# Second attention of a six-layer block: fp32 probabilities as the moving operand over banded fp32 values, and the rotation of queries and keys on GpSimd

## The reference, cut to what matters

```python
q = x @ Wq;  k = x @ Wk;  v = x @ Wv                  # 16 query heads, 4 key/value heads, head width 8
q = _rope(q, cos(ang), sin(ang));  k = _rope(k, cos(angk), sin(angk))
scores = einsum('bhqd,bhkd->bhqk', q, k) / sqrt(128)  # 256 x 256 per head, no mask
p = softmax(scores, axis=-1)
o = einsum('bhqk,bhkd->bhqd', p, v)
return o.transpose(0, 2, 1, 3).reshape(B, S, D) @ Wo
```

## Time and profile before

| | before |
|---|---|
| median of 3 runs | 1822.4 us (1815.99 to 1823.57) |
| profiled execution, span of its instructions | 2151.2 us |
| time of the profiled execution around the span | none is given |
| attention 1: first scores to the last add | 1219.7 to 1595.5 us of the span |
| VectorE / ScalarE / TensorE busy, 1400 to 1444 us | 94% / 85% / 80% |
| granted TensorE clock there | 0.50 |
| GpSimd busy there | 69% |

### The profile page before, as it was taken

The page is one execution under the profiler, slowest core; times in us unless marked ns, Lnnn a source line. Parts: engine busy times, 40 slices in busy tenths (PEclk is TensorE's granted clock), DMA queues, the critical chain, the costliest instruction groups (busy, mean ns, idle before and its releaser), DMA issues.

```text
span 2151.2 us, 34449 instructions
## 1 busy us (share of the span) xinstructions
PE 1289.1 (60%) x11544; PEld 930.5 (43%) x11545; DVE 1132.4 (53%) x2864; ACT 781.4 (36%) x1164; POOL 970.1 (45%) x1052
## 2 busy tenths in 40 slices
PE   2496578736921424987743387777750513997762
PEld 1495466526820113976511144444430201986621
DVE  6445677672478101423533699889978200333442
ACT  1243366613410001533211188888850100443310
POOL 0623155523225764034462267667633766024464
PEclk9997799957955766999775555555555755998885
DMA  7232144102200112444310000000000111444321
GB/s 303 82 88 73 57 159 152 57 12 86 76 25 31 48 67 67 149 137 123 92 48 22 11 2 2 3 2 2 2 1 20 48 66 52 137 141 129 108 74 49
DMA packets 100126, 150.60 MB, mean 70 GB/s; under 512 B 21520, under 2 KB 54928, under 8 KB 99216
## 3 DMA queue, kind: packets, MB, share of 16 engines
q1 hardware_dynamic: 58768, 75.30, 11.0%
q0 software_dynamic: 20480, 41.98, 6.7%
q10 hardware_dynamic: 20736, 31.47, 4.3%
HBM read 74.16 MB, written 74.45 MB: 69 GB/s over the span
## 4 chain that ended last, share of the span: by engine, by line
PE 33%; DVE 19%; another core or an unknown queue 17%; issue 15%; ACT 4%; POOL 4%; SPq 4%; DMA 3%; ACTq 1%; DVEq 0%; POOLq 0%
PE PS L910 6%; PE PS L932 3%; PE PS L847 3%; SPq L1349 2%; PE PS L300 2%; PE PS L302 2%; PE PS L301 2%; PE PS L1793 2%; PE PS L918 2%; POOL AREA L1100 2%; POOL slots_top L626 2%; DVE AREA L1959 2%; DVE X L1123 1%; DVE XN L409 1%
## 5 line engine op out<-in xcount | busy, mean ns | idle before, releaser
L1100 POOL DMA_INDIRECT AREA<-results_top,ROW x320 | 305.3, 954 | 516.5 <-DMA results_top<-AREA 330.1
L626 POOL DMA_INDIRECT slots_top<-XN,ROW x320 | 318.2, 995 | 319.0 <-DVE ROW L580 185.8
L742 DVE SCALAR_TENSOR_TENSOR AREA<-PS,AREA 128x512 f32<-128x512 f32 x64 | 43.8, 691 | 323.2 <-issue 181.2
L910 PE MATMUL PS<-WGU,AREA 128*128 x768 | 192.7, 396 | 13.7 <-ACT AREA L974 13.7
L1754 POOL TENSOR_TENSOR AREA<-AREA 128x1024 f16<-128x1024 f32 x64 | 151.4, 2365 | 91.6 <-ACT AREA L1894 91.4
L1011 DVE SCALAR_TENSOR_TENSOR AREA<-PS,AREA 128x512 f32<-128x512 f32 x96 | 66.4, 692 | 218.0 <-ACT AREA L985 170.9
L712 ACT ACTIVATE AREA<-PS 128x512 f32<-128x512 f32 x64 | 38.1, 598 | 373.7 <-remote 293.9
L1983 DVE TENSOR_REDUCE AREA<-PS 128x4 f32<-128x1024 f32 x128 | 156.1, 1219 | 25.4 <-PE PS L1781 24.7
L1887 ACT ACTIVATE AREA<-PS,AREA 128x1024 f32<-128x1024 f32 x128 | 142.7, 1115 | 53.5 <-PE PS L1793 53.5
L910 PEld LDWEIGHTS PS<-WGU,AREA 128*128 128x128 f32 x768 | 146.3, 201 | 32.9 <-ACT AREA L974 15.0
L932 PE MATMUL PS<-WD,AREA 128*128 x768 | 112.5, 293 | 53.3 <-DVE AREA L1006 46.2
(11 more groups left out here) (261 smaller groups left out, 3636.4 us busy)
## 6 DMA issues: line engine op xcount, KB each, us to landing
AREA<-slots_top SPq DMA_DIRECT2D x96, 256.0 KB
results_top<-AREA ACTq DMA_DIRECT2D x96, 256.0 KB
slots_top<-ZERO SPq DMA_DIRECT2D x24, 512.0 KB, 3.1
AREA<-slots_top SPq DMA_DIRECT2D x48, 128.0 KB
results_top<-AREA ACTq DMA_DIRECT2D x48, 128.0 KB
AREA<-query_rows SPq DMA_DIRECT2D x48, 128.0 KB, 2.9
slots_top<-XN,ROW POOLq DMA_INDIRECT x320
AREA<-results_top,ROW POOLq DMA_INDIRECT x320
```

The lines of the kernel that those rows point to most:

```text
L626: nc.gpsimd.indirect_dma_start(out=L.xs[q], out_offset=bass.IndirectOffsetOnAxis(ap=ROW[:, n:n + 1], axis=0), in_=XN[:, t * D:(t + 1) * D] ...
L910: ins = nc.tensor.matmul(o, XTF[:, v, j * P:(j + 1) * P], w, start=True, stop=True)
L1100: nc.gpsimd.indirect_dma_start(out=slots[L.tag][u][:, c * D:(c + 1) * D], out_offset=None, in_=L.ys[g * GT // L.tiles], in_offset=bass.Ind ...
```

## The change

It touches attention 1 alone.

- The split of the probabilities is gone (`phi`, `plo`, `PB1`). `PF1` is now fp32 and double, one for even and one for odd tiles.
- `values` has the roles swapped: the stationary operand is `V32`, for each of 8 tiles and 4 key/value heads 128 keys x 32 columns in fp32, of which 8 hold v, one holds 1.0 and the rest 0; the moving operand is `PF1`, 256 columns in fp32. Head g writes partitions 32g to 32g+32 of bank 6, so that the four matmuls of a call use four different bands of columns of the array. 16 matmuls for a tile, in four calls, run in the turn after the tile's exponentials.
- The result lies by head and query: ScalarE copies the whole bank (512 columns) to `OS`, TensorE transposes it back in four fp32 transposes (`values_turned`, bank 7), VectorE's `norm` has two operations, one fp32 transpose (into bank 0), a copy to `OT` and one fp32 matmul with Wo (`AOF`, rows in another order) follow. The add to x comes a turn later, and the turns go on for one more.
- `rope` moves from VectorE to GpSimd: ScalarE copies columns 0 to 320 of the projections to `PJQ` (in `XN`, which is free then), and GpSimd does two multiplications and an addition, each part behind a `carry_wait`. ScalarE's copy of v gives it in fp32; there is no low half.

The diff, cut to its core:

```diff
-        PF1 = area([4, 1024], F32)
-        PB1 = [area([4, 1024], F16) for _ in range(2)]
-        OS = area([16 * 17], F32)
+        PF1 = [area([4, 1024], F32) for _ in range(2)]
+        OS = area([4 * P], F32)
+        V32 = area([8, 4, 32], F32)
+        PJQ = XN[:, 0:640].rearrange("p (a b) -> p a b", b=320)
...
-            for c in range(NT - 5, NT + 2):
+            for c in range(NT - 5, NT + 3):
                 turn(0, c)
...
+            def rope(i, c):
+                t = i * 8 + c
+                wait(pool, b_pj, t + 1)
+                wait(pool, b_rope, t)
+                wait(pool, b_pack, t - 1)
+                carry_wait()
+                nc.gpsimd.tensor_tensor(RT[:, 0, :], PJQ[:, c % 2, 0:160], COS[:, c % 2, :], ALU.mult)
+                nc.gpsimd.tensor_tensor(RT[:, 1, :], PJQ[:, c % 2, 160:320], SIN[:, c % 2, :], ALU.mult
+                                        ).then_inc(b_rstep.sem, 1)
+                wait(pool, b_rstep, t + 1)
+                carry_wait()
+                nc.gpsimd.tensor_tensor(RF[:, c % 2, :], RT[:, 0, :], RT[:, 1, :], ALU.add).then_inc(b_rope.sem, 1)
...
                 if tile_exists(i, c + 4):
                     pack_k(i, c + 4)
-                if tile_exists(i, c - 1):
-                    plo(i, c - 1, 3)
-                if tile_exists(i, c + 4):
                     pack_q(i, c + 4)
-                if tile_exists(i, c):
-                    plo(i, c, 1)
+                if tile_exists(i, c + 5):
+                    rope(i, c + 5)
...
-            def values(i, c, g):
+            def values(i, c, n):
                 t = i * 8 + c
-                wait_split(pe, i, c, g)
-                if g == 0:
-                    wait(pe, b_oc, t)
-                for r in range(4):
-                    o = (4 * g + r) * 17
-                    for k in range(2):
...
-                        nc.tensor.matmul(banks(6)[:, o:o + 17], p[0], v, start=k == 0, stop=False)
-                        ins = nc.tensor.matmul(banks(6)[:, o:o + 9], p[1], v[:, 0:9], start=False, stop=k == 1)
+                odd, k = divmod(n, 2)
+                wait(pe, b_exp, 4 * t + 4)
+                wait(pe, b_oc, t)
+                for g in range(4):
+                    at = odd * 512 + k * 256
+                    ins = nc.tensor.matmul(banks(6)[32 * g:32 * (g + 1), odd * 256:(odd + 1) * 256],
+                                           V32[:, (c // 2 * 2 + k) % 8, g, :], PF1[c % 2][:, g, at:at + 256],
+                                           start=k == 0, stop=k == 1)
                 ins.then_inc(b_pv.sem, 1)
+
+            def values_turned(i, c):
+                t = i * 8 + c
+                wait(pe, b_oc, t + 1)
+                wait(pe, b_on, t)
+                for odd in range(2):
+                    for half in range(2):
+                        at, r = (odd * 2 + half) * P, 2 * half + odd
+                        ins = nc.tensor.transpose(banks(7)[:, r * P:(r + 1) * P], OS[:, at:at + P], IDF[:, :])
+                ins.then_inc(b_vt.sem, 1)
...
-                    before = c - 1 if g < 3 else c
-                    if tile_exists(i, before):
-                        values(i, before, (g - 3) % 4)
+                    if g > 0 and tile_exists(i, c - 1):
+                        values(i, c - 1, g - 1)
+                    if g == 3 and tile_exists(i, c - 1):
+                        values(i, c - 1, 3)
...
+                    if g == 1 and tile_exists(i, c - 2):
+                        values_turned(i, c - 2)
+                    if g == 1 and tile_exists(i, c - 3):
+                        wait(pe, b_ot, t - 2)
+                        nc.tensor.matmul(banks(0)[:, 352:480], OT, AOF, start=True, stop=True).then_inc(b_y.sem, 1)
...
-                nc.scalar.activation(PB1[0][:, g, :], PF1[:, g, :], ACT.Copy).then_inc(b_phi.sem, 1)
+            def values_copy(i, c):
+                t = i * 8 + c
+                wait(act, b_pv, 4 * t + 4)
+                wait(act, b_vt, t)
+                nc.scalar.activation(OS, banks(6), ACT.Copy).then_inc(b_oc.sem, 1)
...
+                        nc.scalar.activation(PJQ[:, (c + 5) % 2, :], banks(0)[:, 0:320], ACT.Copy, scale=1.0 / SW
+                                             ).then_inc(b_pj.sem, 1)
```

More of the change, by code:

```diff
@@ L223, in build @@
         AW = [area([352], F16, 0), area([352], F16)]
-        AO = [area([D], F16) for _ in range(2)]
+        AOF = area([D], F32)
         COS, SIN = (area([2, 160], F32) for _ in range(2))
@@ L1869, in turn @@
                         q_four(c + 3, b_q1tr)
-                    if g == 3 and tile_exists(i, c - 2):
-                        wait(pe, b_ot, t - 1)
-                        product3(banks(7)[:, 0:D], [OTB[:, n * P:(n + 1) * P] for n in range(2)],
-                                 [AO[n][:, :] for n in range(2)]).then_inc(b_y.sem, 1)
             tile_turns(pe, turn)
@@ L1957, in plo @@
-            def plo(i, c, g):
-                wait(dve, b_phi, 4 * (i * 8 + c) + g + 1)
-                nc.vector.tensor_tensor(PB1[1][:, g, :], PF1[:, g, :], PB1[0][:, g, :],
-                                        ALU.subtract).then_inc(b_plo[0].sem, 1)
+            dve.wait_ge(*b_whi.at(1))
+            nc.vector.scalar_tensor_tensor(out=AW[1], in0=WST, scalar=SW, in1=AW[0], op0=ALU.mult,
+                                           op1=ALU.subtract).then_inc(b_wlo.sem, 1)
+            dve.wait_ge(*b_cst.at(9))
@@ L1985, in turn @@
                                              ).then_inc(b_max.sem, 1)
-                    if g == 1 and tile_exists(i, c):
-                        plo(i, c, 0)
                     if g == 0 and tile_exists(i, c + 1):
@@ L1998, in turn @@
                     if g == 2 and tile_exists(i, c - 2):
-                        wait(dve, b_otr, t - 1)
-                        wait(dve, b_y, t - 2)
-                        nc.vector.tensor_copy(OTB[:, :], banks(7).bitcast(F16)[:, 0:2 * P]).then_inc(b_ot.sem, 1)
-                    if g == 1 and not last and tile_exists(i, c - 3):
+                        norm(i, c - 2)
+                    if g == 3 and not last and tile_exists(i, c - 3):
                         wait(dve, b_oadd, t - 2)
@@ L2004, in turn @@
                         statistics(t - 3)
-                    if g == 3 and tile_exists(i, c + 5):
-                        rope(i, c + 5)
-                    if g == 3 and tile_exists(i, c - 1):
-                        wait(dve, b_olo, t - 1)
-                        norm(i, c - 1)
-                    if g == 3 and tile_exists(i, c - 2):
-                        wait(dve, b_y, t - 1)
-                        x = X[:, bass.ds((t - 2) * D, D)]
-                        nc.vector.scalar_tensor_tensor(out=x, in0=banks(7)[:, 0:D], scalar=1.0 / (SX * SW), in1=x,
-                                                       op0=ALU.mult, op1=ALU.add).then_inc(b_oadd.sem, 1)
@@ L2027, in moe_counts @@
+        ATTN1_COUNTS.update({s: 4 * NT for s in (b_s, b_max, b_st, b_exp, b_pv)})
         def moe_counts(L):
```

153 lines of the change are left out of this document (53 added, 100 removed).

## The result

| | before | changed |
|---|---|---|
| median of the runs | 1822.3 us | 1761.2 us (1758.8 to 1771.3, four runs) |
| ratio, 95% interval | | 0.9681 (0.9648 to 0.9714) |
| first maximum to last add of attention 1 | 374.8 us | 309.6 us |
| one turn, mean | 11.03 us | 9.06 us |

What follows compares the result with a forecast made beforehand. VectorE, nearest to full, and ScalarE were taken to bound attention 1; afterwards TensorE. 31.75 turns x (11.03 - 9.0) = -64 us, fill +4, end -3, low-clock turns +6: -57, so 1765 us; range 1728 to 1825.

Steps and rivals of the forecast that it cites:

- the fill of the first turns: Start of attention 1: a rotation 1.4 us longer, about three turns that nothing hides, +4 us.
- the step that carried the us over whole: From profile (2151 to 2094 us) to runs' median 1822.4: the 57 us kept whole, giving 1765; shrunk in proportion, 1774.
- I take the middle: `values` on TensorE: second half of a head waits for the first, one record's time a matmul, 16 x 0.216 = 3.5 us.
- the lower bound of the forecast: `values` on TensorE with all four matmuls of a call beside each other: 8 x 0.216 = 1.7 us a tile.
- the slower rival: `values` in steps 1 to 3: no overlap of bands of columns, 6.9 us, turn 12.4, +43 us, 1866; chance 0.13.
- four bands at once: Rival: `values` at 1.7 us, TensorE 6.7, turn 8.2 us set by exponentials and key chain; -89 us, 1733; chance 0.20.
- The clock ... still has 8.4 of 9 us: TensorE's clock in attention 1: rises within the first tiles and, with 8.4 us of work in 9, keeps 1.00.
- the clock falls back: Rival, or key chain late: turns of 10.0 us, half partly at 1.2 GHz; -26 us, 1796; chance 0.18.
- the forecast's own observable: Sign to check: a `values` call about 1.1 us from first start to last end; 0.6 four bands, 1.9 no overlap.
- The term of +6 us for turns before the rise: Start of attention 1: three turns of 15.4 us in place of 9 at the lower clock, less what the fill hides.
- I cost the move at nothing: Rotation on GpSimd: keys ready 3.3 us after the last exponential, TensorE wants them at 3.35 or later; cover gone, 0.5 us a tile.
- VectorE is the nearest to full ... the phase moves only if VectorE and ScalarE lose work: Attention 1 before: VectorE busy 41.33 of 44 us, ScalarE 37.6; VectorE to fall to 6.8 us a tile, ScalarE to 7.0.

Runs made afterwards that it cites:

- the early copies: Changed kernel with ScalarE's copies of the projections and of v ahead of a turn's fourth exponential; 2108.8 us (ratio 0.9604), in a later session 1733.5 us (0.9504).
- one head a call: Changed kernel with each `values` call taking the four matmuls of one head, all in one band of columns; 2211.8 us against 2197.6, ratio 1.0061.
- the added matmuls: Kernel before with an unneeded matmul of 512 columns ahead of `scores` in each of the four steps; 1918.9 us, ratio 1.0538.

## Why the prediction was right

The time (1761 for 1765), the side, the turn (9.06 for 9.0), the fill of the first turns (from the last weights' copy to the first maximum 2.3 us longer, +4 predicted), the end (10.8 to 8.6 us from last exponential to last add, -3 predicted) and the step that carried the us over whole (-63.5 at a level of 1822; the early copies gave -88.8 at 2198 and -88.4 at 1822) all held, some only roughly. VectorE and ScalarE came out at 6.2 and 6.0 us a turn (68 and 67% of 9.06), where 6.8 and 7.0 had been counted: the durations were added up, but neighbours overlap by some 0.1 us (the exponential above lasts until 1204.98, the copy behind it starts at 1204.87). For the same reason the maxima, `plo` and "3.6 us of small things" come to 11.6 us, more than the turn, where VectorE is busy for 10.3. The chances are off by a hundredth (0.13 and 0.07 for slower are 0.20). But the turn came out right by luck, because two terms were wrong in opposite directions.

**"I take the middle", `values` at 3.5 us a tile.** The step held that the second record of an fp32 matmul blocks the band behind it, so that a matmul costs one record's time. Measured: 0.43 us a further call, 1.7 us a tile, the lower bound of the forecast. Both records of each matmul overlap with those of the other three bands; with one head a call, a call costs 1.71 us, the upper bound. The Trainium skill (TensorE: Matmul & The Clock Gate, "Measured speedup vs the span model") had pointed there, with 2.38 times for three bands (its table does not name the type of the matmuls); these runs show about 4 times for four. Its "What overlaps and what doesn't", quoted for the slower rival, speaks of weight loads; here the eight loads of a call use the same 128 rows as the matmuls, take 0.11 us each, 0.9 in sum, and fit into its 0.43 us: they overlap matmuls in the same rows, which that sentence excludes. The rival "four bands at once" named the mechanism and gave a turn of 8.2 us; the short turns are 8.4.

**"The clock ... still has 8.4 of 9 us", so stays at 1.00.** With `values` at 1.7, TensorE has 6.7 us of work in an 8.4 us turn, and idles 0.6 and 0.4 us close together in step 0. The clock did rise where expected, at the start of the third turn (after 5.00 of 5 us busy), but falls again in 12 of the 22 turns, 1.3 us each. That is the rival "the clock falls back", priced there at 1.0 us a turn against 9.0; against the true 8.4 it was 0.7. The two errors, -0.6 and +0.7 us a turn, cancelled: the forecast's own observable, 1.1 us for a call, would have shown it (0.64). The term of +6 us for turns before the rise came out at +2.8: two such turns, of 9.9 and 10.9 us, not three of 15.4.

**"I cost the move at nothing."** Of the move of the rotation, the part that the prediction followed was right: keys ready 3.3 us after the last exponential (1204.98 to 1208.27), wanted at about that time; TensorE waits 8.6 us for them in 18 turns, under the 0.5 us a turn set as the bound. The part that it noted and did not follow was ScalarE's order: "ahead of `QT1`, whose reader comes a turn later". But the next turn's first `scores` is ready to start 0.5 us after that exponential (1205.5 against 1204.98). It waits for `QT1` in 25 turns, and moving the two copies gave 25 us. So the move, costed at nothing, cost some 15 us as it was made (-63.5 against -78 with the rotation on VectorE, in different sessions).

**"VectorE is the nearest to full ... the phase moves only if VectorE and ScalarE lose work."** Not shown: TensorE at 1.2 GHz stood on the chain too, as the added matmuls showed, and the rotation moved alone took too little off VectorE, and gave too much to the others, to tell. The change helped all three at once. Which of them alone would have sufficed, no run separates. And the mean of 11.03 held the two pauses, some 6.5 us, which the forecast took for work of the engines: that they would end was no part of its reasoning.

The gain hangs on the clock. TensorE in the second turn of the changed kernel, still at 1.2 GHz, in which the transposes back and Wo are not yet due:

```profile
1048.38 0.61 PE L1794 MATMUL PS<-AREA 32*128 32x256 f16 x4 [0.87 <-ACT AREA L1899]
...
1057.45 1.94 PE L1807 MATMUL PS<-AREA 128*32 128x256 f32 x16
1059.32 0.39 PE L1794 MATMUL PS<-AREA 32*128 32x256 f16 x4
```

Two calls of `values` take 1.94 us, and the turn 10.9; with the missing work it would be no shorter than the 11.03 of before. So I read it that the new form pays only at 2.4 GHz; no run held it at 1.2.

## What to carry to other kernels

Write small fp32 products so that neighbouring matmuls go to different bands of columns: here this alone was the difference between 61 to 63 us gained and 14 us lost. When an edit adds an operation, follow every later instruction of that engine in the program to its reader, above all where the reader stands at the start of the next turn, and put the addition into the engine's idle time ahead of it. After an edit that makes TensorE the chain, read the granted clock in stretches of a turn or less, and shorten or fill the gap ahead of each fall before anything else.

## What the runs showed of the hardware that was not expected

- Each further call of four fp32 matmuls of 256 columns, eight records, takes 0.43 us in four bands of columns, two records' time; in one band 1.7 us.
- A useless matmul of 0.39 us a turn made the kernel 20.4 us faster (1738.0 against 1758.4), most of it through the clock.
- The clock falls for some 3 us at a time behind gaps of 0.6 and 0.4 us in a phase where TensorE is 86% busy; yet it never rose in the kernel before, nor with 2.2 us a turn of matmuls added there, at 80% busy.
- The kernel before took 1822 or 2198 us, the one with early copies 1734 or 2109, in different sessions. In the two profiles of the latter, GpSimd's wait for result stores (the group of L1099) is 90 against 355 us, and turns of attention 1 without a fall are alike, 7.94 to 8.13 us.
- In the kernel before TensorE and VectorE pause twice for about 3 us, eight turns apart, waiting for nothing that the profile shows; kernels with the new `values` have no such pause.
